# Chunk-by-chunk splitting of Wq and Wk, and their product with the contraction outside

## What is computed

```python
Pn = rmsnorm(P, input_norm_w)
k_proj = Pn @ Wk.T
v_proj = Pn @ Wv.T
for _ in range(3):
    sn = rmsnorm(slots, slot_norm_w)
    q_proj = sn @ Wq.T
    scores = einsum('bkd,bmd->bkm', q_proj, k_proj) * SCALE
    attn = softmax(scores, axis=-2)
    attn = attn / (sum(attn, axis=-1) + EPS)
    updates = einsum('bkm,bmd->bkd', attn, v_proj)
    slots = gru_cell(updates, slots, gru_wih, gru_whh, gru_bih, gru_bhh)
```

## Time and profile before

| | us |
|---|---|
| median of 3 runs | 935.09 |
| lowest and highest | 931.84, 937.68 |
| the profiled execution | 930.46 |
| its span in the trace | 928.7 |
| its mean granted TensorE clock | 0.933 |

### The profile page before, as it was taken

How to read it: one execution, slowest core, us unless ns; L and a number is a source line. 1 busy time by engine, 2 the same in 40 slices (tenths; PEclk the granted TensorE clock), 3 DMA queues, 4 the chain that set the end, 5 groups by cost and what they waited for, 6 DMA issues and landing times. The chain is left out here.

```text
span 928.7 us, 37863 instructions
## 1 busy us (share of the span) xinstructions
PE 773.4 (83%) x17278; PEld 645.3 (69%) x17278; DVE 599.4 (65%) x1146; ACT 364.7 (39%) x726; POOL 162.1 (17%) x431
## 2 busy tenths in 40 slices
PE   3598679998989998989997989978589787659995
PEld 1445669998978997978997978878545665324442
DVE  2777447784775785876775875645565787893225
ACT  3577414432444433534333531111247664452221
POOL 3020210402130411220411220201001103240003
PEclk9899789999999999989999999989879798879998
DMA  9947990227093336092346091510394711454424
GB/s 340 357 103 140 233 203 4 55 55 201 5 162 145 55 61 196 15 192 103 54 65 192 12 178 52 110 32 13 127 354 117 233 25 24 155 168 96 126 80 147
DMA packets 179419, 115.75 MB, mean 125 GB/s; under 512 B 145788, under 2 KB 158132, under 8 KB 176060
## 3 DMA queue, kind: packets, MB, share of 16 engines
q1 hardware_dynamic: 168272, 100.85, 43.0%
q10 hardware_dynamic: 8988, 6.69, 2.4%
q0 software_dynamic: 2000, 5.80, 2.1%
HBM read 61.94 MB, written 12.85 MB: 81 GB/s over the span
## 5 line engine op out<-in xcount | busy, mean ns | idle before, releaser
L1021 PE MATMUL banks<-qa,ctxT 128*128 128x64 f16 x3744 | 121.5, 195 | 22.0 <-issue 12.8
L1021 PEld LDWEIGHTS banks<-qa,ctxT 128*128 128x128 f16 x3744 | 117.6, 100 | 24.4 <-issue 14.2
L972 PEld LDWEIGHTS banks<-wall,whhT 128*128 128x128 f16 x3456 | 111.7, 100 | 15.9 <-issue 8.8
L972 PE MATMUL banks<-wall,whhT 128*128 128x64 f16 x3456 | 114.0, 195 | 9.0 <-issue 7.5
L972 PE MATMUL banks<-qa,wall 128*128 128x64 f16 x3456 | 104.9, 193 | 3.1 <-DVE qa L783 2.8
L972 PEld LDWEIGHTS banks<-qa,wall 128*128 128x128 f16 x3456 | 102.5, 98 | 3.4 <-DVE qa L783 3.0
L1040 PE MATMUL banks<-qa,wall 128*128 128x64 f16 (+1 forms) x1872 | 92.5, 198 | 8.4 <-issue 6.7
L1040 PEld LDWEIGHTS banks<-qa,wall 128*128 128x128 f16 (+1 forms) x1872 | 91.6, 102 | 9.4 <-issue 9.4
L1040 PE MATMUL banks<-wall 128*128 128x64 f16 (+1 forms) x936 | 91.3, 198 | 2.1 <-issue 2.1
L1040 PEld LDWEIGHTS banks<-wall 128*128 128x128 f16 (+1 forms) x936 | 86.6, 102 | 1.9 <-issue 1.9
L88 POOL TENSOR_TENSOR wall<-wall 128x64 f32<-128x64 f32 x24 | 12.3, 512 | 363.7 <-DVE wall L83 363.7
(11 more groups left out here) (280 smaller groups left out, 1495.6 us busy)
## 6 DMA issues: line engine op xcount, KB each, us to landing
wall<-in_ctx_dram SPq DMA_DIRECT2D x17, 1024.0 KB, 10.3
wall<-in_L_ffn_routed_w_dram SPq DMA_DIRECT2D x23, 512.0 KB, 8.2
unit<-in_ctx_dram SPq DMA_DIRECT2D x6, 1024.0 KB, 7.6
xg_scratch<-room SPq DMA_DIRECT2D x1, 3840.0 KB, 20.3
y_scratch<-room ACTq DMA_DIRECT2D x15, 256.0 KB, 2.1
ctxT<-in_L_xattn_gru_wih_dram SPq DMA_DIRECT2D x3, 1024.0 KB, 17.5
ctxT<-in_L_xattn_gru_whh_dram SPq DMA_DIRECT2D x1, 3072.0 KB, 25.9
ctxT<-in_L_attn_Wqkv_dram SPq DMA_DIRECT2D x12, 256.0 KB, 8.0
```

What stands on the lines that cost most here:

```text
L972: mm = pe.matmul(dst[o], a, b, start=start, stop=True, skip_group_check=True)
L1021: mm = pe.matmul(score[n][:, t * K:(t + 1) * K], a, q, start=(k == 0), stop=(k == 3 * DC - 1), skip_group_check=True)
```

## The change

Wq and Wk are each split in four pieces of 128 x 512 (chunk ec of the contraction), alternating between the two, on ACT and on DVE. PE takes chunk 0 as soon as its two pieces are split and makes from it the first three passes of all four rows of A, in four banks (`a_bank`: two of score[1], two of score[0]), then chunk 1, and so on: `a_rows` instead of four calls of `a_row`. The number of matmuls stays 48. All four rows are complete only in the last chunk. Read-out on DVE is written in another order: `a_row(f)` keeps only the scaling, `a_low(f)` the subtraction. Wv is split ahead of all read-outs and not behind the first, with an additional wait of ACT, since its halves overwrite the raw Wk. The `bn_stats` of x stand behind all read-outs and not between them. PE has one additional wait (`folded_f32`, 4) ahead of `x_turned`, whose banks now held rows of A. The wait of SP ahead of the context of batch 1 has another count for the same event (Wv's low half).

```diff
--- before.py
+++ after.py
@@ -234,6 +234,9 @@
         def fold_bank(f):
             return score[1][:, 512 * (f % 2):512 * (f % 2) + 512]
 
+        def a_bank(f):
+            return score[1 - f // 2][:, 512 * (f % 2):512 * (f % 2) + 512]
+
         def turn_bank(t):
             return gate[1 - t % 4 // 2][:, t % 2, :]
 
@@ -374,7 +377,7 @@
             load_wih(2)
             sp.dma_start(whh_halves[:, 2:2 * GC + 2].rearrange("p s d -> p (s d)").bitcast(F32).rearrange("p (c d) -> p c d", c=GC),
                          dram.gru_whh.rearrange("(c p) d -> p c d", p=P)).then_inc(whh_in, 16)
-            sp.wait_ge(qkv_split, 3)
+            sp.wait_ge(qkv_split, 2 * DC + 1)
             load_context(1, (0, 1))
 
             sp.wait_ge(turned, GC)
@@ -476,12 +479,8 @@
 
         @block.scalar
         def _(act):
-            def raw_high(j):
-                if j == 0:
-                    act.wait_ge(wqk_in, 32)
-                if j == 2:
-                    act.wait_ge(wv_in, 16)
-                act.activation(wqkv_s[j][:, 0], wqkv_raw[j], ACT.Copy, scale=WS).then_inc(qkv_hi, 1)
+            def raw_high(j, ec):
+                act.activation(wqkv_s[j][:, 0, ec], wqkv_raw[j][:, ec], ACT.Copy, scale=WS).then_inc(qkv_hi, 1)
 
             def a_row(f):
                 act.wait_ge(folded_f32, f + 1)
@@ -611,11 +610,14 @@
                     for t in range(DONE):
                         x_high(act, big, e.psum[:, x_bank_of[t]], t)
 
-            raw_high(0)
-            raw_high(1)
-            a_row(0)
-            raw_high(2)
-            for f in range(1, DC):
+            act.wait_ge(wqk_in, 32)
+            for ec in range(DC):
+                for j in range(2):
+                    raw_high(j, ec)
+            act.wait_ge(wv_in, 16)
+            act.wait_ge(qkv_split, 2 * DC)
+            act.activation(wqkv_s[2][:, 0], wqkv_raw[2], ACT.Copy, scale=WS).then_inc(qkv_hi, 1)
+            for f in range(DC):
                 a_row(f)
             for t in range(4):
                 turned_block(t)
@@ -658,11 +660,10 @@
         def _(dve):
             st = Steps(dve, dve_done)
 
-            def split_raw(j):
-                src = wqkv_raw[j].rearrange("p c d -> p (c d)")
-                hi, lo = (wqkv_s[j][:, n].rearrange("p c d -> p (c d)") for n in range(2))
-                dve.wait_ge(qkv_hi, j + 1)
-                dve.scalar_tensor_tensor(lo, src, WS, hi, ALU.mult, ALU.subtract).then_inc(qkv_split, 1)
+            def split_raw(j, ec):
+                dve.wait_ge(qkv_hi, 2 * ec + j + 1)
+                dve.scalar_tensor_tensor(wqkv_s[j][:, 1, ec], wqkv_raw[j][:, ec], WS, wqkv_s[j][:, 0, ec], ALU.mult, ALU.subtract)\
+                    .then_inc(qkv_split, 1)
 
             def turned_block(t):
                 dve.wait_ge(turned_hi, t + 1)
@@ -673,8 +674,11 @@
                 dve.wait_ge(folded, f + 1)
                 if f >= 2:
                     dve.wait_ge(folded_hi, f - 1)
-                dve.scalar_tensor_tensor(f32row[:, f % 2], fold_bank(f), w_slot[:, f:f + 1], w_in_row,
+                    dve.wait_ge(folded_lo, f - 1)
+                dve.scalar_tensor_tensor(f32row[:, f % 2], a_bank(f), w_slot[:, f:f + 1], w_in_row,
                                          ALU.mult, ALU.mult).then_inc(folded_f32, 1)
+
+            def a_low(f):
                 dve.wait_ge(folded_hi, f + 1)
                 dve.tensor_tensor(fold_dst(f, 1), f32row[:, f % 2], fold_dst(f, 0), ALU.subtract).then_inc(folded_lo, 1)
 
@@ -861,26 +865,30 @@
                 slots_low(1, r + 1)
                 chunk_sums(1, r + 1)
 
-            split_raw(0)
-            split_raw(1)
+            for ec in range(DC):
+                for j in range(2):
+                    split_raw(j, ec)
             dve.wait_ge(vecs_turned, 1)
             dve.tensor_scalar(vecs[:], gate[1][:, 1, 0:2 * DC], 1.0 / WS, None, ALU.mult).then_inc(vecs_out, 1)
+            dve.wait_ge(qkv_hi, 2 * DC + 1)
+            dve.scalar_tensor_tensor(wqkv_s[2][:, 1], wqkv_raw[2], WS, wqkv_s[2][:, 0], ALU.mult, ALU.subtract).then_inc(qkv_split, 1)
             dve.wait_ge(vecs_out, 1)
             dve.wait_ge(small_in, 16)
             a_row(0)
-            split_raw(2)
+            a_row(1)
+            a_low(0)
+            a_row(2)
+            a_low(1)
+            a_row(3)
+            a_low(2)
+            a_low(3)
             dve.wait_ge(x_in, 16)
-            for t in range(2):
-                st(dve.bn_stats(e.stats[:, t], xr[:, t]))
-            a_row(1)
-            for t in range(2, RT):
+            for t in range(RT):
                 n = st(dve.bn_stats(e.stats[:, t], xr[:, t]))
             st.after(n)
             for t in range(RT):
                 n = st(dve.bn_aggr(e.mv[:, t], e.stats[:, t]))
             st.after(n)
-            a_row(2)
-            a_row(3)
             for t in range(4):
                 turned_block(t)
             normalise(dve, st, xr, xr, e.mv, ln_small, xn_ready)
@@ -947,12 +955,19 @@
                         n += 1
                 mm.then_inc(folded, 1)
 
-            def a_row(f):
-                fold(f, lambda i, ec: wqkv_s[0][:, i, ec, f * P:(f + 1) * P], lambda i, ec: wqkv_s[1][:, i, ec, :])
+            def a_rows():
+                for ec in range(DC):
+                    pe.wait_ge(qkv_split, 2 * (ec + 1))
+                    for f in range(DC):
+                        passes = split_passes(lambda i: wqkv_s[0][:, i, ec, f * P:(f + 1) * P], lambda i: wqkv_s[1][:, i, ec, :])
+                        for m, (a, b) in enumerate(passes):
+                            mm = pe.matmul(a_bank(f), a, b, start=(ec == 0 and m == 0), stop=(ec == DC - 1 and m == 2))
+                        if ec == DC - 1:
+                            mm.then_inc(folded, 1)
 
             def b_row(f):
                 g, dc = divmod(f - DC, DC)
-                pe.wait_ge(qkv_split, 3)
+                pe.wait_ge(qkv_split, 2 * DC + 1)
                 pe.wait_ge(turned_lo, DC * (g + 1))
                 fold(f, lambda i, ec: wqkv_s[2][:, i, ec, dc * P:(dc + 1) * P], lambda i, ec: wihT[:, i, ec, g * D:(g + 1) * D])
 
@@ -1091,12 +1106,11 @@
             pe.wait_ge(consts_done, 3)
             pe.wait_ge(vec_in, 32)
             pe.transpose(gate[1][:, 1, 0:2 * DC], vec_rows, c.ident32[0:2 * DC, 0:2 * DC]).then_inc(vecs_turned, 1)
-            pe.wait_ge(qkv_split, 2)
-            for f in range(DC):
-                a_row(f)
+            a_rows()
             pe.wait_ge(vecs_out, 1)
             for t in range(8):
                 turn(t)
+            pe.wait_ge(folded_f32, DC)
             for t in range(RT):
                 x_turned(t)
             for t in range(8, GC):
```

## The result

The changed kernel is faster by 0.8%: the ratio to the kernel before is 0.9923, with a 95% interval of 0.9902 to 0.9944. The median of 16 runs is 925.1 us (917.64 to 934.21), that of 16 runs of the kernel before beside it 931.54 (926.54 to 942.46), so 6.4 us by the medians and 7.2 by the ratio. The ratio leaves out one slow execution of each kernel (934.21 and 942.46), which took over 1.5% longer than the fastest of the same kernel. The forecast was a gain of 6.7 us.

What follows compares the result with a forecast made beforehand. The opening was taken as bound by PE's product, then DVE, then ACT. Terms -4.5 and -2.4 for PE, of it -4.6 at DVE, with ACT's 2 us lag -6.7: median 935.09 to 928.4, range 923.0 to 933.5.

Steps and rivals of the forecast that it cites:

- Step 1: Split of Wq and Wk: eight pieces cost DVE 5.2 us, PE starts at 11.2 instead of 15.75, 4.5 us earlier.
- Step 2: PE's product for A: 48 matmuls in one run without the inner wait, done at 23.5, 7.0 us earlier.
- my bounds: PE's product: 1.8 us less if all matmuls ran at the later pace, about 1.7 more if the slow start doubled.
- Step 3: DVE's read-outs and statistics: row 0 at 21.6, gru_wih's first low half at 30.3 instead of 34.86, 4.6 us earlier.
- Step 4: ACT through gru_wih: PE's fifth block at 31.0, ACT goes on at 31.75, x_out near 36.1; 6.7 us earlier.
- the sum: Whole opening: -4.5 start and -2.4 inner wait for PE's product, -4.6 for DVE at gru_wih, -6.7 for the chain.
- Step 5: Loads: same order, gru_wih's second third there at 29.85, wanted at 31.0, 1.1 us of slack; costed at nothing.
- Only DVE's 4.6: x's turning or gru_wih's first half slips by 2 us, so only 4.6 us arrives: 930.5; chance 0.15.
- Half-pace rows of B: Clock drops after PE's longer idling; one row of B at half pace leaves -4.2 us, two -1.7; chance 0.12.
- Slower: Whole kernel slower than before, from three half-pace rows of B on (935.9); chance 0.06, over 1% slower 0.03.
- late load: gru_wih's second third lands after 31.0, each us beyond is lost: 930 to 933; chance 0.05.
- dear pieces: Split pieces cost DVE so much that the product's last chunk starts later than 20.9: 935; chance 0.03.

Runs made afterwards that it cites:

- e3: The changed kernel with PE waiting for all eight pieces before its first matmul; ratio to the kernel before 0.9975.
- e5: The changed kernel itself profiled and timed once more, with no edit; ratio to the kernel before 0.9921.
- e7: e2 with the statistics of x behind the read-outs, as the change has them; ratio to the kernel before 0.9961.
- e1: The kernel before with only A's four rows put in four banks, so PE makes all 48 matmuls in one run; ratio 1.0011.
- e2: The kernel before with only DVE's and ACT's order changed: Wv split first, subtractions later, statistics of x between rows; ratio 0.9963.
- e4: The changed kernel with the statistics of x ahead of Wv's low half on DVE; ratio to the kernel before 0.9923.
- e6: e4 with PE making chunks 0 and 1 for all rows, then chunks 2 and 3 row by row; ratio to the kernel before 0.9903.
- e8: The kernel before with only the split in eight pieces, PE still waiting for all of them; ratio 1.0023.
- e9: The changed kernel with the old read-out order on ACT and DVE (pieces, chunks outside and four banks kept); ratio to the kernel before 0.9994.

## Why the prediction was right, and where its reasons were not

One relation fits all eleven profiles to 0.05 us. ACT needs 4.37 us from S to T (four high halves, four squares), and T cannot come sooner than 1.96 us behind L (DVE's first low half, PE's fifth block, both 1.96 in the changed kernel, e3, e5 and e7). Both numbers are read from these profiles; what the relation adds is that the same two hold in all of them. So T is the later of S + 4.37 and L + 1.96:

| | S + 4.37 | L + 1.96 | T |
|---|---|---|---|
| before | 38.49 | 36.82 | 38.49 |
| changed | 31.05 | 32.28 | 32.28 |
| e1 | 38.57 | 36.89 | 38.57 |
| e2 | 34.00 | 32.33 | 34.00 |
| e3 | 35.33 | 36.57 | 36.57 |
| e4 | 31.06 | 29.39 | 31.06 |
| e5 | 31.72 | 32.95 | 32.95 |
| e6 | 30.56 | 28.88 | 30.61 |
| e7 | 34.24 | 35.48 | 35.48 |
| e8 | 38.23 | 36.56 | 38.23 |
| e9 | 40.82 | 39.14 | 40.82 |

From T to R it is 21.03 to 21.08 us in seven of the eleven, and 20.21 to 20.24 in the four others: the changed kernel, e4, e5 and e6. The difference of 0.83 is seen where PE turns x. Timelines of PE and ACT before:

```profile
43.62 1.94 PE L964 MATMUL banks<-ident,wall 128*128 128x128 f32 x8 [2.47 <-ACT whhT L501]
```

```profile
44.74 0.58 ACT L501 COPY whhT<-banks 128x512 f32<-128x512 f32 x1 [0.78 <-PE banks L964]
45.59 0.58 ACT L501 COPY whhT<-banks 128x512 f32<-128x512 f32 x1 [0.27 <-PE banks L964]
```

The last eight transposes of x took 1.94 us, with the granted clock at 0.89 and 0.68 of its higher level in the stretches around (40 to 44, 44 to 48), and ACT waited 0.78 and 0.27 for them. They took 1.94 in e1, e2, e7, e8 and e9 too; in e3 all sixteen took 3.80. In the changed kernel the last eight took 1.11 (1.12 in e4, e5 and e6), at 1.00 in the stretch from 36 to 40, and ACT waited 0.32. Why the clock was up at this point in these four and not in e3, which has the same program but for the start, no run shows.

Between B's first row and R there is one more wait that the change doesn't touch. POOL works out the row norms of the context in ten small instructions; ACT waits 2.87 us for them, before and after, and DVE 2.81 us for ACT. Timeline of ACT after the change:

```profile
49.44 1.33 ACT L528 ACTIVATE wall<-wall,rrow 128x512 f16<-128x512 f32 x2 [2.87 <-POOL rrow L97]
```

Point by point:

- **Step 1, the split.** Right: PE at 11.23 for 11.2, eight pieces in 4.90 us for 5.2. The Trainium skill's fixed cost per instruction ("VectorE: DVE Perf Modes", section on the TRN2 errata) is there and small: 4.90 against 4.49 us, hidden.
- **Step 2, the product.** Right: done at 23.4 for 23.5, with some luck, since the same kernel took 12.57 us and not 12.18 in e5. That a cycling through PSUM banks costs clock, as the Trainium skill has it ("TensorE: Matmul & The Clock Gate", "A second HAM failure mode: psum-queue depth-cycling"), the traces do not show: four banks row by row took 12.06 (e1), four banks chunk by chunk 12.18 to 13.42, two banks without a wait 12.57 (e2, e7). The spread lies in how long the start ran at half pace, which my bounds held.
- **Step 3, DVE.** Right to 0.1 in each number: F 21.62 for 21.6, L 30.32 for 30.3.
- **Step 4, ACT.** T came at 32.28 for 31.75: the fifth block behind L cost 1.96 us and not 1.45. PE starts it 0.84 behind L, and ACT goes on 1.12 after that, where I had 0.7 and 0.75 (16 transposes in 3.65 us, half pace). x_out came at 36.66 for 36.1. Up to here the gain was 6.2 us and not 6.7. The 0.83 us at x, which I had not in the sum, gave it back: R 52.49 for 52.8. That was luck: by its own terms the sum was worth 6.2.
- **Step 5, the loads.** Right: ACT had Wv at 16.05 for 15.95, and from there to R no DMA ended a wait. The slack of gru_wih's second third was real, since e4 ran into its landing at 29.65.
- **Where the reasons failed is the sum.** "-4.5 (start) - 2.4 (inner wait) = -7.0 for PE's product; of it -4.6 for DVE" reads as if PE's 7 us were the source (and 4.5 and 2.4 make 6.9). e1 (PE's wait removed: +0.07) and e9 (PE done 6 us earlier: +2.33) show that it is not. The 6.7 itself was taken from step 4's way through L, not from these two terms, and so it held. DVE's 4.54 is F later by 1.25 and F to L shorter by 5.79 (14.49 to 8.70): Wv's 2.29 and its wait of 1.12 taken out of the way, and three of the four gaps of 0.68 filled, 2.0; the remaining 0.4 is small change between instructions. What the chunks and the early start do is to let all four rows be complete by 23.4 and not by 30.5, so that this shorter read-out can end in time: S is 26.68 with them and 29.6 without (e2). The two halves of the change need each other. In T, which the clock at x doesn't touch, the read-outs alone give 4.5 (e2) or 3.0 with the statistics where the change has them (e7), the chunks alone lose 2.3 (1.2 of it the order, in e9), and together they give 6.2.
- **The rivals.** Only DVE's 4.6: no, though e2's gain of 4.5 is of this size, for another reason. Half-pace rows of B: none, 84 matmuls in 18.29 us in every kernel. Slower, late load, dear pieces: no. That the gain of the opening arrives at the end held: R by -7.0, the wait for whh by -7.4, the ratio by -7.2. The wait for whh is good to about 1 us in a single profile, as e4 shows. The remaining 1.3 of the span's 8.7 I can't attribute.

A version with the latest markers earlier (e6) points on: its fifth block waits for a load and its ACT is busy from S to T, so this part of the opening is now held by ACT's own work, with the bytes ahead of gru_wih's second third close behind. Behind B's first row the 2.87 us that ACT waits for POOL come next; no run tried them.

## What to carry to other kernels

When a product is read out by a chain of two engines, price the chain behind the first finished row, not only the product: here PE was done 6 us earlier for nothing as long as the read-out kept its order (e9). Turning the contraction outside starts the product earlier but finishes its first row last, so it pays only where the read-outs behind that row are short, and the reader's other work has been moved into the time in which it would wait. Mark three or four instants on each engine and compare these between kernels; at 1% of the time they say more than the time does, once a second profile of the same kernel has shown how far they scatter.

## What the runs showed that I had not expected

The product's 48 matmuls took 12.06 to 13.42 us in nine profiles of nearly the same code, and the matmuls in each 4 us show the difference in the start: 20 in a stretch once it is over, 10 to 14 in the first whole one, and in e9 still 17 in the second. From PE's start to F it is 10.39 to 11.63 us in the five profiles with the chunks of the change (changed, e3, e4, e5, e9), so that start is worth up to 1.2 us of F. And eight small transposes of x at the lower clock (1.94 us against 1.11) cost ACT 0.83 us, three times the 0.24 by which the split in pieces alone moved R (e8).
